# Eight layers on one core: the third feed-forward with centred second weights, statistics on VectorE, the additions to x on GpSimd, and a three-part up product

## What is computed

```python
def _L2_ffn_ref(x, gate_w, w1, b1, w2, b2, ln_g, ln_b):
    E, K, D = (8, 2, 128)
    ...
    xt = x.reshape(-1, orig_shape[-1])
    scores = xt @ gate_w
    ew, ei = jax.lax.top_k(scores, K)
    ew = jax.nn.softmax(ew, axis=-1)
    mask = ei[None, :, :] == jnp.arange(E)[:, None, None]
    wE = jnp.sum(ew[None, :, :] * mask, axis=-1)
    h = jax.nn.gelu(jnp.einsum('td,edf->etf', xt, w1) + b1[:, None, :], approximate=False)
    o = jnp.einsum('etf,efd->etd', h, w2) + b2[:, None, :]
    y = _layernorm(xt[None, :, :] + o, ln_g[:, None, :], ln_b[:, None, :])
    out = jnp.einsum('et,etd->td', wE, y)
    return out.reshape(orig_shape)
```

## Time and profile before

| what | value |
|---|---|
| median of 3 runs | 1144.24 us (1136.63 to 1147.08) |
| the profiled execution, its own time | 1135.98 us |
| its span, first to last instruction | 1134.2 us |
| mean granted TensorE clock | 0.888 of full |
| busy over the whole span | PE 917.4, DVE 677.8, ACT 433.0, POOL 550.0 us |
| first up product of the third feed-forward | 639.7 us from the span's start |
| last down product ends | 777.4 us |
| next normalisation of x begins | 799.4 us |

### The profile page before, as it was taken

How to read it: one execution, slowest core, us unless ns; L and a number is a source line. 1 busy time by engine, 2 the same in 40 slices (tenths; PEclk the granted TensorE clock), 3 DMA queues, 4 the chain that set the end, 5 groups by cost and what they waited for, 6 DMA issues and landing times. The chain is left out here.

```text
span 1134.2 us, 18018 instructions
## 1 busy us (share of the span) xinstructions
PE 917.4 (81%) x6494; PEld 592.5 (52%) x6494; DVE 677.8 (60%) x1706; ACT 433.0 (38%) x876; POOL 550.0 (48%) x430
## 2 busy tenths in 40 slices
PE   4559999999989878267999899994699997299993
PEld 2113333333333446164566676663697667199883
DVE  6756667767660255979677479999302475643334
ACT  2334665566555422014111356665344211032221
POOL 4335977897788611152312158888300001146661
PEclk9658999999997988658799699998799998599997
DMA  5700111011000000001000000030200000166665
GB/s 169 222 1 2 29 30 30 2 29 30 3 1 23 1 21 8 9 6 56 2 1 2 1 10 20 19 128 0 75 1 1 1 10 29 55 191 214 211 206 143
DMA packets 37815, 56.40 MB, mean 50 GB/s; under 512 B 5643, under 2 KB 25091, under 8 KB 37607
## 3 DMA queue, kind: packets, MB, share of 16 engines
q1 hardware_dynamic: 35238, 50.21, 14.5%
q0 software_dynamic: 2496, 5.12, 1.6%
HBM read 44.17 MB, written 10.94 MB: 49 GB/s over the span
## 5 line engine op out<-in xcount | busy, mean ns | idle before, releaser
L671 DVE TENSOR_REDUCE arena<-ps 128x2 f32<-128x1024 f32 (+2 forms) x192 | 177.3, 955 | 86.9 <-PE ps L487 55.5
L420 POOL TENSOR_TENSOR arena<-arena 128x1024 f32<-128x1024 f32 (+3 forms) x105 | 201.3, 1957 | 38.8 <-ACT arena L606 38.8
L606 ACT ACTIVATE arena<-ps 128x512 f32<-128x512 f32 (+3 forms) x320 | 138.8, 489 | 91.4 <-PE ps L519 57.6
L117 POOL TENSOR_SCALAR vareps<-meanvar 128x4 f32<-128x4 f32 x32 | 7.8, 245 | 234.6 <-DVE meanvar L98 234.6
L511 PE MATMUL ps<-arena 51*128 51x512 bf16 (+3 forms) x384 | 91.4, 345 | 18.0 <-ACT arena L606 6.8
L152 PE MATMUL ps<-ident,xn 128*128 128x128 f32 x128 | 27.2, 365 | 69.2 <-DVE xn L106 25.4
L511 PEld LDWEIGHTS ps<-arena 51*128 51x128 bf16 x384 | 26.9, 94 | 106.9 <-ACT arena L606 59.7
L2058 PE MATMUL ps<-arena 128*128 128x128 f32 x624 | 78.1, 279 | 0.0
L1389 PEld LDWEIGHTS ps<-arena 128*128 128x128 f32 x512 | 60.8, 192 | 30.7 <-ACT arena L1443 20.3
L2058 PEld LDWEIGHTS ps<-arena 128*128 128x128 f32 x624 | 74.6, 196 | 0.0
L420 POOL TENSOR_TENSOR xnT<-xnT,arena 128x1024 f32<-128x1024 f32 (+1 forms) x28 | 52.8, 1907 | 42.1 <-ACT xnT L606 42.1
(11 more groups left out here) (319 smaller groups left out, 1985.7 us busy)
## 6 DMA issues: line engine op xcount, KB each, us to landing
arena<-in_L_ffn_w SPq DMA_DIRECT2D x39, 512.0 KB, 4.2
arena<-scratch SPq DMA_DIRECT2D x32, 192.0 KB, 3.9
scratch<-arena SPq DMA_DIRECT2D x12, 256.0 KB, 3.9
arena<-in_L_ffn_w SPq DMA_DIRECT2D x8, 257.0 KB, 2.7
arena<-in_L_ffn_w SPq DMA_DIRECT2D x8, 256.0 KB, 4.0
arena<-expert_rows SPq DMA_DIRECT2D x8, 256.0 KB, 4.8
scratch<-arena SPq DMA_DIRECT2D x4, 384.0 KB, 5.1
scratch<-arena SPq DMA_DIRECT2D x12, 128.0 KB, 4.2
```

Source lines behind the costliest of these rows:

```text
L420: nc.gpsimd.tensor_tensor(e, e, weight[:, at:at + k].unsqueeze(1).broadcast_to([P, 2, k]), ALU.mult).then_inc(weighed, 1)
L606: nc.scalar.activation(probs(g)[:, 2 * p + e, 0:wd], m.ps[:, BANK[h, e], 0:wd], ACT.Exp, scale=SCALE).then_inc(exps, 1)
L671: nc.vector.tensor_reduce(out, scores, AX.X, ALU.max, negate=True).then_inc(max_set, 1)
```

## The change

All of it is in `l2_ffn`.

- The second weights are centred: VectorE sums each row of an expert's second weights (`sum_weights`), and GpSimd subtracts the mean (`split_weights`). The second bias is centred as well, and the normalised x has mean zero, so z needs no shift: the minus-mean instruction and ScalarE's four shift-and-scale instructions are gone.
- The second bias enters as one float32r matmul in a down product (`pick` by `b2_rows`), and not through `xb`.
- The up product is three float32r matmuls for each half: x is split by `split_xnT`, the first weights by `round_weights` (ScalarE) and `split_weights` (GpSimd).
- VectorE takes mean and variance of a step directly one behind the other; GpSimd adds epsilon, takes the power and multiplies by the router weight (`wrs`); VectorE multiplies z by `wrs` and the gain at once (`scale`), two steps late; GpSimd adds the result `y` to x (`add`).
- All 32 steps are written out. The transposed weights are made in step 4 and the norm's bias is added in steps 5 and 6; TensorE no longer waits for the router's first copy before it begins.

The two places at which the prediction looks are shown in the engines' order. First GpSimd, about the steps of the middle experts. Before, a round of the loop: the power (L1477), `xb` (L1466) and the gain (L1470); ISA and REGISTER_ALU rows set addresses.

```diff
...
+    STEPS = E * NC
+    m.rounded.fresh()
+    x_high, x_low = norm.split_xnT()
+    w = sb("l2f_w", [P, 2, 2 * F])
+    w1_high, w1_low = (m.rounded.take(f"l2f_w1_{n}", [P, 2, F], F32R) for n in ("high", "low"))
+    w2c = sb("l2f_w2c", [P, 2, FT, D])
+    w2_mean = sb("l2f_w2_mean", [P, 2, FT])
...
+    b2_rows = m.rounded.take("l2f_b2_rows", [P, D], F32R)
+    b2_mean, is_high, is_low = (sb(f"l2f_{n}", [2 * E, 1]) for n in ("b2_mean", "is_high", "is_low"))
+    pick = m.rounded.take("l2f_pick", [P, E, P], F32R)
...
+        for e in range(E):
+            if e >= 2:
+                sp.wait_ge(w1_low_set, e - 1)
+                sp.wait_ge(w2_centred, e - 1)
+            sp.dma_start(w[:, e % 2, :], A["L2_ffn_w"][e, :, 0:2 * F]).then_inc(w_in[e % 2], 16)
...
+        def up(n):
+            e, c = divmod(n, NC)
+            cs = slice(c * CH, (c + 1) * CH)
             if c == 0:
-                pe.wait_ge(w_in[u], (i + 1) * 16)
-            if n is None or n >= 2:
-                pe.wait_ge(h_done, i * (FT * UNROLL) + FT * (k - 1))
+                pe.wait_ge(w1_low_set, e + 1)
+            if n >= 2:
+                pe.wait_ge(h_done, FT * (n - 1))
             for f in range(FT):
...
+                fs = slice(f * P, (f + 1) * P)
+                out = m.ps[:, 2 * (n % 2) + f, :]
+                nc.tensor.matmul(out, w1_high[:, e % 2, fs], x_high[:, cs], start=True, stop=False)
+                nc.tensor.matmul(out, w1_high[:, e % 2, fs], x_low[:, cs], start=False, stop=False)
+                nc.tensor.matmul(out, w1_low[:, e % 2, fs], x_high[:, cs], start=False, stop=True).then_inc(up_done, 1)
...
+        def down(n):
+            e, c = divmod(n, NC)
+            if n == 0:
+                pe.wait_ge(b2_set, 1)
+                pe.wait_ge(step, 1)
+            if c == 0:
+                pe.wait_ge(w2_centred, e + 1)
+            if n >= 2:
+                pe.wait_ge(z_done, n - 1)
+            nc.tensor.matmul(m.ps[:, 4 + n % 2, :], pick[:, e, :], b2_rows[:, :].unsqueeze(1).broadcast_to([P, TPC, D]), start=True, stop=False,
+                             skip_group_check=True)
             for f in range(FT):
+                pe.wait_ge(h_done, FT * n + f + 1)
                 for j in range(TPC):
-                    mm = nc.tensor.matmul(m.ps[:, 4 + k % 2, j * P:(j + 1) * P], hT[:, k % 2, f, j * P:(j + 1) * P],
-                                          w[:, u, W2 + f * P:W2 + (f + 1) * P], start=(f == 0 and j == 0),
-                                          stop=(f == FT - 1), skip_group_check=True)
+                    mm = nc.tensor.matmul(m.ps[:, 4 + n % 2, j * P:(j + 1) * P], hT[:, n % 2, f, j * P:(j + 1) * P], w2c[:, e % 2, f, :],
+                                          start=False, stop=(f == FT - 1), skip_group_check=True)
...
+        for n in range(STEPS):
+            up(n)
+            if n:
+                down(n - 1)
+            if n == 4:
+                turn_weights()
+            if n == 6:
                 norm_biases()
-
-        pipelined(pe, body, lambda: down(E // 2 - 1, UNROLL - 1, None))
+        down(STEPS - 1)
...
+        def round_weights(e):
+            act.wait_ge(w_in[e % 2], 16 * (e // 2 + 1))
+            if e >= 2:
+                act.wait_ge(up_done, FT * NC * (e - 1))
+            nc.scalar.activation(w1_high[:, e % 2, :], w[:, e % 2, W1:W1 + F], ACT.Copy).then_inc(w1_high_set, 1)
+
+        round_weights(0)
         norm.copy_xnT(act, NC - 1)
...
+                if n >= 2:
+                    act.wait_ge(o_done, n - 1)
+                nc.scalar.activation(hT[:, n % 2, f, :], m.ps[:, 2 * (n % 2) + f, :], ACT.Gelu, bias=b1[:, e, f:f + 1]).then_inc(h_done, 1)
             if n == 1:
+                act.wait_ge(step, 2 + RANK_STEPS)
+                nc.scalar.activation(gap[:, :], gap[:, :], ACT.Exp).then_inc(exps, 1)
...
+        def split_weights(e):
+            pool.wait_ge(w1_high_set, e + 1)
+            if e >= 2:
+                pool.wait_ge(up_done, FT * NC * (e - 1))
+            nc.gpsimd.tensor_tensor(w1_low[:, e % 2, :], w[:, e % 2, W1:W1 + F], w1_high[:, e % 2, :].bitcast(F32), ALU.subtract).then_inc(w1_low_set, 1)
+            pool.wait_ge(w2_summed, 2 * e + 2)
+            if e >= 2:
+                pool.wait_ge(o_done, NC * (e - 1))
+            for f in range(FT):
+                ins = nc.gpsimd.tensor_scalar(w2c[:, e % 2, f, :], w[:, e % 2, W2 + f * D:W2 + (f + 1) * D], w2_mean[:, e % 2, f:f + 1], None, ALU.subtract)
+            ins.then_inc(w2_centred, 1)
+
+        def add(n):
+            c = n % NC
+            pool.wait_ge(y_set, n + 1)
+            if n >= NC:
+                pool.wait_ge(y_done, n - NC + 1)
+            if n == NC - 1:
+                pool.wait_ge(lnb_added, NC)
+            xs = m.x[:, c * TPC:(c + 1) * TPC, :]
+            nc.gpsimd.tensor_tensor(xs, y[:, n % 2, :, :], xs, ALU.add).then_inc(y_done, 1)
+
+        split_weights(0)
+        for n in range(STEPS):
+            e, c = divmod(n, NC)
+            if n >= 4:
+                pool.wait_ge(y_set, n - 3)
+            pool.wait_ge(var, n + 1)
+            nc.gpsimd.tensor_scalar(ve[:, n % 4, :], mv[:, n % 4, :, 1], EPS, None, ALU.add).then_inc(scales, 1)
+            pool.wait_ge(scales, 3 * n + 1)
+            nc.gpsimd.tensor_tensor(rs[:, n % 4, :], ve[:, n % 4, :], m.power[:, 0:TPC], ALU.pow).then_inc(scales, 1)
+            pool.wait_ge(scales, 3 * n + 2)
+            if n == 0:
+                pool.wait_ge(wte_set, 1)
+            nc.gpsimd.tensor_tensor(wrs[:, n % 4, :], rs[:, n % 4, :], wte[:, c * TPC:(c + 1) * TPC, e], ALU.mult).then_inc(scales, 1)
+            if n >= 2:
+                add(n - 2)
+            if c == 1 and e + 1 < E:
+                split_weights(e + 1)
+        add(STEPS - 2)
+        add(STEPS - 1)
...
+        def sum_weights(e):
+            dve.wait_ge(w_in[e % 2], 16 * (e // 2 + 1))
+            if e >= 2:
+                dve.wait_ge(w2_centred, e - 1)
+            nc.vector.tensor_reduce(w2_mean[:, e % 2, :], w[:, e % 2, W2:W2 + F].rearrange("p (f d) -> p f d", d=D), AX.X, ALU.add).then_inc(w2_summed, 1)
+            dve.wait_ge(w2_summed, 2 * e + 1)
+            nc.vector.tensor_scalar(w2_mean[:, e % 2, :], w2_mean[:, e % 2, :], 1.0 / D, None, ALU.mult).then_inc(w2_summed, 1)
...
+        def sums(n):
+            c = n % NC
+            if n >= 3:
+                dve.wait_ge(y_set, n - 2)
+            dve.wait_ge(o_done, n + 1)
+            nc.vector.tensor_tensor(z[:, n % 3, :, :], m.ps[:, 4 + n % 2, :].rearrange("p (j d) -> p j d", d=D), m.xn[:, c * TPC:(c + 1) * TPC, :],
...
+
+        def scale(n):
+            e, c = divmod(n, NC)
+            dve.wait_ge(scales, 3 * n + 3)
+            if n >= 2:
+                dve.wait_ge(y_done, n - 1)
             for j in range(TPC):
...
+                ins = nc.vector.scalar_tensor_tensor(out=y[:, n % 2, j, :], in0=z[:, n % 3, j, :], scalar=wrs[:, n % 4, j:j + 1], in1=lng[:, e, :],
+                                                     op0=ALU.mult, op1=ALU.mult)
+            ins.then_inc(y_set, 1)
...
+        for n in range(STEPS):
+            e, c = divmod(n, NC)
+            sums(n)
+            if n == 1:
+                weights()
+            if n >= 2:
+                scale(n - 2)
+                if n - 3 >= STEPS - NC:
+                    after(dve, n - 3 - (STEPS - NC))
+            if n == 5:
+                dve.wait_ge(y_done, NC - 1)
+                for k in range(NC):
+                    add_biases(k)
                 dve.wait_ge(lnb_added, NC)
...
+            if c == 1 and e + 1 < E:
+                sum_weights(e + 1)
+        for n in (STEPS - 2, STEPS - 1):
+            scale(n)
+            after(dve, n - 1 - (STEPS - NC))
+        after(dve, NC - 1)
...
```

More of the change, by code:

```diff
@@ L1353, in pipelined @@
-    def pipelined(eng, body, tail):
-        for k in range(UNROLL):
-            body(0, k, k)
-        with eng.Fori(1, E // 2) as i:
-            for k in range(UNROLL):
-                body(i, k, None)
-        tail()
+        sp.dma_start(b1[:, :, :], A["L2_ffn_w"][:, :, B1:B1 + FT].rearrange("e p n -> p e n")).then_inc(small_in, 16)
+        for e in range(E):
[3 more added lines that the diff above has]
+            sp.dma_start(w[:, e % 2, :], A["L2_ffn_w"][e, :, 0:2 * F]).then_inc(w_in[e % 2], 16)
@@ L1376, in up @@
             for f in range(FT):
-                mm = nc.tensor.matmul(m.ps[:, 2 * (k % 2) + f, :], w[:, u, W1 + f * P:W1 + (f + 1) * P], m.xnT[:, c * CH:(c + 1) * CH],
-                                      start=True, stop=True)
-                mm.then_inc(up_done, 1)
-        def down(i, k, n):
-            u = k // NC % 2
-            if n is None or n >= 2:
-                pe.wait_ge(z_done, i * UNROLL + (k - 1))
-            pe.wait_ge(h_done, i * (FT * UNROLL) + FT * (k + 1))
+                fs = slice(f * P, (f + 1) * P)
@@ L1567, in add_biases @@
```

(29 more changed lines are left out.)

178 lines of the change are left out of this document (58 added, 120 removed).

## The result

The changed kernel takes **1149.54 us** (median of 20 runs, 1144.02 to 1156.43), the kernel before, run beside it, 1144.45 (20 runs, 1136.63 to 1148.09). The ratio is **1.0050, with a 95% interval from 1.0033 to 1.0067**. It is 0.5% slower, some 5.7 us. I had forecast a gain of 1.0 us, no change. The time lies between the bounds that I gave, but the direction is wrong: the whole interval lies above 1.

The account below looks back on a forecast made before the run. VectorE was taken to bound the kernel, with TensorE held at its pace. The stage's terms gave -4.4 us without clock falls, -1.0 with two; from 1140.4 that made 1140 us, no change, range 1127 to 1152.

Parts of the forecast that it names:

- VectorE's and GpSimd's load: Work per expert of four steps in the loop: VectorE 13.5 us, against 16.4 before, and GpSimd 13.8 us.
- TensorE: TensorE's own work in the loop: 3.40 us a step, 0.1 less than before, so 13.6 us an expert.
- The wait that the change adds: Each expert's first up product waits 2.6 us for GpSimd's split of its weights; an expert takes 16.2 us.
- Start: Stage start: first up product at about 642.5 us, 3.0 later, and up(8) at 682.8, bounds 680 and 687.
- Middle and tail: Five experts at 16.2 us, then 15.6 from last down product to next normalisation, before 22.0; it starts at 795.0.
- TensorE's clock: Falls to half clock behind the waits of five experts: two taken, at 1.7 us each.
- my base: Time of the kernel before to which the sum was set: 1140.4 us, the middle of four known times.
- (a): Rival: the line through GpSimd is shorter and TensorE is never held; -17.4, 1123 us, chance 0.17.
- (c): Rival: VectorE's scalings are held by GpSimd's additions to x; +13.0, 1153 us, chance 0.12.
- no scaling is longer than 0.4: Sign of the forecast in the changed profile: no scaling (L1591) on VectorE takes longer than 0.4 us.
- (d): Rival: the tail gives nothing, GpSimd's additions and powers following each other there; +5.4, 1146 us, chance 0.08.
- (b): Rival: TensorE's clock falls at each expert's wait; +4.1, 1145 us, still no change, chance 0.13.

Follow-up runs that it names:

- e9: The kernel that splits the weights before the addition, with VectorE's scalings in step (e, 1) held until GpSimd's epsilon, power and router weight finish; stage 9.0 us longer than that kernel's.
- e11: The changed kernel with ten extra matmuls, whose result nobody reads, filling TensorE's wait before experts 3 to 7, run once more; ratio 0.9988 to the kernel before.
- e12: The changed kernel with five extra matmuls, whose result nobody reads, in TensorE's wait before experts 3 to 7; ratio 0.9975 to the kernel before.
- e2: The changed kernel with the rounding and split of the next expert's first weights one step earlier, in step (e, 0); 1.0% faster than the kernel before.
- e3: The changed kernel without any split of x and first weights, its up product the float32 matmul of the kernel before; 0.8% faster than the kernel before.
- e1: The changed kernel with GpSimd's split of the next expert's first weights ahead of the addition to x in step (e, 1); ratio 0.9953 to the kernel before.
- e5: The changed kernel with ten extra matmuls, whose result nobody reads, in TensorE's wait before experts 3 to 7, first run; ratio 0.9994 to the kernel before.
- e4: The changed kernel with ten extra matmuls, whose result nobody reads, ahead of TensorE's wait for experts 2 to 7; ratio 1.0057 to the kernel before.

## Why the prediction was wrong, by its own steps

**VectorE's and GpSimd's load**: right. Per expert VectorE works 13.4 us (67.16 / 5) and GpSimd 13.6 (68.13 / 5), where I had summed 13.5 and 13.8. An expert takes 16.7 all the same.

**TensorE**: right. A step is 3.40 us (687.71 to 691.11).

**The wait that the change adds** was right in place and kind: TensorE waits for the split, 2.87 us per expert where I had 2.6, and nowhere else in the loop. But its line was 0.5 us short: 16.74 for 16.2. From the timeline above, start to start, epsilon is 0.51 (I had 0.31), power 1.33 (1.06), the router weight 0.15 (0.25), the addition 1.22 (1.29), the split 0.78 up to the product (0.74 and a handover). The first two are 0.47 over, and e9 shows that the scalings beside them cause 0.4 of it. The rest is the handovers: z begins 10.56 us behind the first up product, where 10.3 and a handover of 0.08 were due, and 0.16 pass from the variance to epsilon, against 0.08. Five experts: 2.7 us.

**Start**: up(0) came at 640.78, 1.7 earlier than forecast, but 1.5 of that is the execution, whose normalisation began earlier; the split of x cost 2.6 us where I had 3.0. Up(8) came at 684.30, 1.5 later, inside the bounds of 680 and 687. Up(4) came 16.9 us behind up(0), where I had 17.1; from it to up(8) it took 26.6 where my sum left 23.2, 3.4 more. I had taken the wait at the norm's biases (1.82), but not that the clock falls behind it: the second half of those products took 3.57 us against 2.05 for the first, and the step behind them 5.07 against 3.40.

**Middle and tail**: right. The tail is 15.1 us, forecast 15.6, before 22.0.

**TensorE's clock** is the largest miss, 3.8 us. I took two falls at 1.7 us, 3.4. There are three in each of three profiled executions, at 1.5 to 2.9 each, 7.2 in the one shown. The two rows of before pointed either way. The standstill in the one behind which the clock stayed was 2.18 us, shorter than these 2.87, and that difference I passed over. And I priced a fall at half of 3.4 us, where two of the three lasted 6.8.

The sum, with what was measured: forecast start of the next normalisation 795.0 without falls; + 1.5 for the start, + 2.7 for the line, + 7.2 for the falls, + 0.3 for the last steps, - 0.5 for the tail = 806.2; it is 806.15.

So the steps that failed are three sizes in a right mechanism: the falls (3.4 forecast, 7.2 measured), the line of an expert (16.2 forecast, 16.74 measured) and the start. The sum had -4.4 without falls. With the falls alone put right it is +2.8, with everything else alone put right, 4.0 us, it is +3.0: either would have turned the sign. That the loss goes when the falls go (e11, e12) fits: -4.4 and 4.0 leave next to nothing. The time itself was about 10 us over the forecast, and 4 of those are my base, 1140.4, where 20 runs of the kernel before gave 1144.45.

**Rivals.** (a), no wait, is false: 14.3 us of it in five. (c), scalings held by the additions, is false as a bound: in the loop the four take 1.10 to 1.14 us, except once per expert, where they meet the split and the centring (1.86 at 700.27), and VectorE waits for TensorE all the same. But my sign "no scaling is longer than 0.4" did not hold: the longest is 1.16 us, the one at 700.27 took 0.84, and in the tail four took 1.95, behind an addition that had begun 0.25 earlier (796.13, scalings from 796.38). What (c) describes, a scaling held by an addition, happens, but only there. (d) is false by the tail. (b), a fall at each wait, was the nearest in time (1145 us, +4.1 against my middle), and its mechanism right for three of five. In the loop the additions run beside VectorE's statistics, not beside its scalings (699.02 and 699.07 above), and there neither holds the other. The rule of the Trainium skill (SBUF — State Buffer, section "SBUF: two separate sides") would price only what meets. Where a scaling met GpSimd's subtraction, at 700.27, the trace agrees with it. It does not agree where the scalings met GpSimd's centring, epsilon and power, which read SBUF too: they ran at the same time, and the scalings were not held (epsilon and power took 0.2 us longer each).

## What to carry to other kernels

When a step moves to another engine, write out the line from one buffer's release to its next use through all engines, and compare it with each engine's load: here it was 3 us longer than any of them. Count what the change does ahead of the stage too, before two variants are compared by the stage (e2 and e3). Whatever in that line is not needed for its end (an addition of an older step, 1.28 us) goes behind it, and what can be done early (the split) goes a step ahead: these changes of order were worth 0.8 to 1.5%. A wait of TensorE costs twice where the clock falls behind it (here 1.5 to 2.9 us more behind three of five), so count that in, and look at stretches at half clock before judging an edit.

## What the runs showed of the hardware

- Behind standstills of TensorE of 2.9 us the granted clock fell to 0.50 at three of five, in three executions, not always the same ones. Behind those of 1.6 to 1.7 us (e1, e12) it did not in two profiles with five each. With 2.35 us at most (e9) it fell once in the loop. A fall lasted 3.4 or 6.8 us. The length of one standstill does not decide it alone: behind the 1.82 us at the norm's biases the clock fell in the changed kernel, e1 and e12 alike, and in the kernel before it fell behind standstills of 0.97, 0.88 and 0.69 us, the last ending at 624.23; the same three in the changed kernel (621.86, 623.20) had no fall right behind them.
- GpSimd's instructions on four numbers a partition took longer beside VectorE's scalings: 0.43 in place of 0.23 us, 1.25 in place of 1.04.
- Four scalings took 1.11 us beside those, but were held by GpSimd's large operations on two tensors. Of the 1.86 us at 700.27, the first 0.69 lie before the split's end (700.96); the rest, 1.17, is about what four take, and lies beside the centring (one tensor and one number a partition), which held nothing. In e9_scale_behind:

```profile
716.19 1.28 POOL L1489 TENSOR_TENSOR x<-arena,x 128x512 f32<-128x512 f32 x1
...
717.03 1.39 DVE L1596 SCALAR_TENSOR_TENSOR arena<-arena 128x128 f32<-128x128 f32 x4
```

  The addition ends at 717.47, and 0.95 us of the scalings' 1.39 are left behind it.
- Extra products at full clock cost nothing in a wait (16.72 to 16.78 us an expert in e5, e11 and e12), and 2.4 us where they fell into a stretch at half clock (e4).
